# Reordering the first steps, the layer change and the end of a two-layer conditioned attention kernel

## The chip, the cores and the metric

The kernel runs on one core of a Trainium2 chip. The metric is the time of one execution in microseconds (us) on the device, the median of several runs. A profiled execution of the same program gives the trace from which all rows below are read.

## What is computed

`x` has shape (32, 128, 512): 32 sequences of 128 tokens with 512 features, in float32. Two layers follow each other, each with its own weights (16 heads of 32 in layer 0, 8 heads of 64 in layer 1). Of one layer:

```python
xn = layernorm(x) * norm_scale + norm_bias
q, k, v = xn @ Wq + bq, xn @ Wk + bk, xn @ Wv + bv
k, v = masked(k), masked(v)
q = softmax(q, within each head)          # over the head's features
k = softmax(k, over the 128 tokens)
attn = einsum('bhse,bhsd->bhed', k, v)
y = einsum('bhtd,bhed->bhte', q, attn)
scale, shift = split(silu(cond) @ film_W + film_b)     # cond: (32, 1024)
h = (layernorm(y) * film_norm_scale + film_norm_bias) * (1 + scale) + shift
x = x + silu(h) @ W_out + b_out
```

All large products run as three float32 products of high and low parts (`WH*XH`, `WL*XH`, `WH*XL`), so that each projection of one sequence is 12 matmuls of 128x512.

## The kernel before

One *step* is one sequence of one layer; there are 64 (0 to 31 in layer 0, 32 to 63 in layer 1). `x` stays in SBUF (`X`). Every engine has its own program, written out by hand as calls of small helpers (`keys(i)`, `values(i)`, `queries(i)`, `attention(j)`, `mix(j)`, `output(o)` on TensorE, and so on); semaphores tie them together. **The order of the calls on an engine is the order of the work**: an instruction that waits holds up everything behind it on its engine. Steps 5 to 30 and 34 to 61 run in loops of `even_step` and `odd_step`; steps 0 to 4, the change of layer (31 to 33) and the end (62, 63) are written out call by call.

What a step does, engine by engine: TensorE makes keys, values and queries; ScalarE keeps the keys in `SK` (`keep_keys`); VectorE takes the maxima over tokens of the keys of two steps (`key_maxima`, and `row_maxima`, which writes `NM`). SyncE sends `NM` to memory (`write_max`, `k_maxima<-NM`) and reads it back on all 128 partitions (`spread_max`, `MX<-k_maxima`, 512 KB); GpSimd subtracts it (`shift_keys`), ScalarE takes the exponential (`exp_k`), and TensorE can do `attention`. VectorE scales its result (`scale_heads`, `HT`), GpSimd puts it on a block diagonal (`heads`, `ATT`), and TensorE multiplies the queries with it (`mix`). The result is normalised (`mixed`, `root_y`, `norm_y`), turned by a DMA to memory and back (VectorE `turn_y`, SyncE `write_qy`/`read_qy`, `qy_turned`, `QT`; the queries travel in the same buffers), passed through `film` on ScalarE and `h_mul` on VectorE, split in two parts (`h_high` on ScalarE, `h_low` on GpSimd) and multiplied with the output weights (`output`). `add_bo` on GpSimd adds the output bias to `X`. The inputs of a pair of steps are normalised on ScalarE (`norm_x`, which needs `stat_x` on VectorE and `root_x` on GpSimd), turned by a DMA (`write_x`, `read_x`, `x_turned`, `XT`), and split (`x_turned` on ScalarE, `x_low` on GpSimd). The tiles `XS` and `QS` are what VectorE turned; they are free again when their DMA to memory has landed.

Weights are split in two parts by `split_high(w, chunks)` on ScalarE and `split_low` on VectorE or GpSimd; `w` is 0 to 3 for keys, values, queries and output of layer 0, 4 to 7 for layer 1. The weights of layer 1 come through one buffer, `STAGE`, chunk by chunk: a chunk is loaded (`load_second`) once the chunk before it has been split (`low_w`). `load_w(3)` brings the output weights of layer 0 (`in_wo`, 1 MB) and `load_film(0)` and `load_film(1)` the two halves of its conditioning weights (`in_film`, 2 MB each). They stand on SyncE's queue with the small transfers of each step. The product with the condition is `conditioning(n)`, `conditioning_sums(n)` and `conditioning_fold(n)`; `conditioning_fold` multiplies by `FOLD`, which `start()` on VectorE makes, with the head masks `DG`.

## Time and profile before

| | us |
|---|---|
| median of 3 runs | 910.99 (910.52 to 911.63) |
| the profiled execution | 909.31 |
| its span in the trace | 907.5 |
| TensorE busy | 847.9 |
| VectorE busy | 679.1 |
| GpSimd busy | 615.1 |
| ScalarE busy | 553.3 |

The profiled execution's time is 1.8 us above its span, and the median of the runs 1.7 us above that time. A timeline row gives the start and the duration of an instruction, and in brackets how long its engine had been idle before it and what ended that. "issue" there means that the trace names no other engine for the end of the wait. Where durations of matmuls are given, they overlap a little: twelve matmuls of 128x512 take 2.7 to 2.9 us when the granted clock is 1.00 (2.4 GHz) and some 5 us when it is 0.50 (1.2 GHz).

### The profile page before, as it was taken

The page shows a single profiled execution, that of the slowest core. Times are in us where ns is not written, and L with a number is a line of the kernel's source. Part 1 is how long each engine was busy: PE and PEld are TensorE (multiplying, and loading weights), DVE is VectorE, ACT ScalarE, POOL GpSimd, SP SyncE. Part 2 cuts the span into 40 slices and gives each one's busy share as a digit, 9 for nine tenths or more (in the row PEclk, how much of TensorE's full clock was granted, in tenths as well). Part 3 has the DMA queues.
Part 4 walks back from the last instruction along what each step waited for, and adds up shares of the span by engine and source line. Part 5 has one row for each costly group of instructions (what it writes and reads, how often), then busy time and mean ns, then how long its engine had stood idle before and what let it go on. Part 6 is the DMA issues. An engine that isn't in the chain of part 4 may idle for free.

```text
span 907.5 us, 18202 instructions
## 1 busy us (share of the span) xinstructions
PE 847.9 (93%) x5923; PEld 690.2 (76%) x5923; DVE 679.1 (75%) x1367; ACT 553.3 (61%) x994; POOL 615.1 (68%) x833
## 2 busy tenths in 40 slices
PE   8967799999999999999966989999999999999997
PEld 7645578787878877888745878888878787887876
DVE  6945568878878797888675678778877777877765
ACT  6245456666666666666663666666676666666653
POOL 2356457777767777777645787778776777777661
PEclk9988889999999999999989999999999999999999
DMA  9725246554555655444374345445454555445331
GB/s 349 239 90 164 93 135 207 191 182 164 183 191 163 209 186 178 149 153 149 119 222 135 96 141 187 159 168 174 159 170 139 174 172 178 157 170 186 117 106 59
DMA packets 94307, 148.85 MB, mean 164 GB/s; under 512 B 10990, under 2 KB 63590, under 8 KB 94214
## 3 DMA queue, kind: packets, MB, share of 16 engines
q1 hardware_dynamic: 93584, 146.97, 49.2%
q8 instruction: 48, 0.79, 0.4%
q10 hardware_dynamic: 630, 0.73, 0.2%
q14 instruction: 45, 0.37, 0.1%
HBM read 91.43 MB, written 56.23 MB: 163 GB/s over the span
## 4 chain that ended last, share of the span: by engine, by line
PE 59%; POOL 10%; DMA 9%; issue 8%; DVE 7%; ACT 5%; SPq 2%; POOLq 0%; ACTq 0%; DVEq 0%
PE PS L1126 51%; PE PS L1221 4%; DMA qy_turned<-QS 3%; DMA QT<-qy_turned 2%; PE PS L1196 2%; POOL SK L651 2%; ACT Z L854 2%; DMA X<-in_wq 1%; POOL XL L644 1%; POOL X L628 1%; SPq L448 1%; POOL SQ L635 1%; DMA MX<-k_maxima 1%; POOL RSY L593 1%; DMA k_maxima<-NM 1%
## 5 line engine op out<-in xcount | busy, mean ns | idle before, releaser
L854 ACT ACTIVATE Z<-QT,FC,FA 128x128 f32<-128x128 f32 x240 | 99.0, 483 | 74.8 <-DMA QT<-qy_turned 74.8
L1126 PE MATMUL PS<-WH_o,HH 128*128 128x512 f32 x248 | 101.1, 408 | 18.2 <-issue 18.2
L673 POOL TENSOR_TENSOR HL<-H,HH 128x512 fp32r<-128x512 f32 x60 | 77.9, 1298 | 57.1 <-ACT HH L896 55.6
L665 POOL TENSOR_TENSOR ATT<-HT,DG 128x256 f32<-128x256 f32 x124 | 76.8, 640 | 57.8 <-DVE HT L1596 30.0
L1126 PE MATMUL PS<-WH_v,XH 128*128 128x512 f32 x256 | 104.8, 409 | 9.9 <-DVE VV L1626 8.9
L1126 PE MATMUL PS<-WH_k,XH 128*128 128x512 f32 x256 | 107.0, 418 | 4.7 <-POOL XL L644 2.9
L1126 PE MATMUL PS<-WH_q,XH 128*128 128x512 f32 x256 | 101.1, 395 | 2.4 <-DVE SQ L1610 2.4
L1126 PE MATMUL PS<-WL_v,XH 128*128 128x512 f32 x256 | 101.8, 398 | 0.0
L1126 PE MATMUL PS<-WH_v,XL 128*128 128x512 f32 x256 | 101.6, 397 | 0.0
L1126 PE MATMUL PS<-WL_k,XH 128*128 128x512 f32 x256 | 101.2, 395 | 0.0
L1126 PE MATMUL PS<-WH_k,XL 128*128 128x512 f32 x256 | 100.8, 394 | 0.0
L1126 PE MATMUL PS<-WL_q,XH 128*128 128x512 f32 x256 | 99.9, 390 | 0.0
L1126 PE MATMUL PS<-WH_q,XL 128*128 128x512 f32 x256 | 99.7, 389 | 0.0
L1126 PE MATMUL PS<-WH_o,HL 128*128 128x512 f32 x248 | 98.8, 398 | 0.0
L1126 PE MATMUL PS<-WL_o,HH 128*128 128x512 f32 x248 | 98.7, 398 | 0.0
L644 POOL TENSOR_TENSOR XL<-XF,XH 128x512 fp32r<-128x512 f32 x60 | 77.6, 1294 | 30.7 <-ACT XH L922 29.1
L651 POOL TENSOR_TENSOR SK<-SK,MX 128x512 f32<-128x512 f32 x64 | 81.5, 1295 | 16.1 <-DMA MX<-k_maxima 16.0
L818 ACT ACTIVATE SK<-SK 128x512 f32<-128x512 f32 x64 | 40.3, 632 | 79.7 <-POOL SK L651 79.5
L635 POOL TENSOR_TENSOR SQ<-SQ,QM 128x512 f32<-128x512 f32 x64 | 67.9, 1061 | 29.5 <-DVE QM L1614 28.1
L823 ACT ACTIVATE YN<-YN,NBY,RSY 128x512 f32<-128x512 f32 x61 | 49.8, 816 | 61.0 <-POOL NBY L616 61.0
L628 POOL TENSOR_TENSOR X<-X,BB 128x512 f32<-128x512 f32 x64 | 82.6, 1292 | 2.3
L1221 PE MATMUL PS<-ATT,EQ 128*128 128x132 f32 x512 | 70.5, 282 | 13.1 <-issue 9.5
(174 smaller groups left out, 2060.2 us busy)
## 6 DMA issues: line engine op xcount, KB each, us to landing
qy_turned<-QS SPq DMA_DIRECT2D x60, 512.0 KB, 3.1
QT<-qy_turned SPq DMA_DIRECT2D x240, 128.0 KB, 2.9
MX<-k_maxima SPq DMA_DIRECT2D x32, 512.0 KB, 3.6
x_turned<-XS SPq DMA_DIRECT2D x30, 512.0 KB, 2.7
XT<-x_turned SPq DMA_DIRECT2D x120, 128.0 KB, 2.9
out_x<-X SPq DMA_DIRECT2D x31, 256.0 KB, 2.9
X<-in_x SPq DMA_DIRECT2D x11, 512.0 KB, 4.3
X<-in_film SPq DMA_DIRECT2D x2, 2048.0 KB, 13.0
```

The lines of the kernel that those rows point to most:

```text
L628: eng.tensor_tensor(X[:, b, :], X[:, b, :], BB[:, 2, :], ALU.add).then_inc(pool_bo, 1)
L635: eng.tensor_tensor(sq, sq, QM[:, 0:D // w].unsqueeze(2).to_broadcast([P, D // w, w]), ALU.subtract)\
L644: eng.tensor_tensor(XL[g % 2][:, dst, :], XF0[:, :, :], XH[g % 2][:, dst, :].bitcast(F32), ALU.subtract).then_inc(pool_xl, 1)
L651: eng.tensor_tensor(sk, sk, MX[:, i % 2, :], ALU.subtract).then_inc(pool_kn, 1)
L665: last = eng.tensor_tensor(dst, src.to_broadcast([P, 2, P // w, w]), here.to_broadcast([P, 2, P // w, w]), ALU.mult)
L673: eng.tensor_tensor(hl_of(o), h_of(o), hh_of(o).bitcast(F32), ALU.subtract).then_inc(pool_hl, 1)
L818: eng.activation(sk, sk, ACT.Exp).then_inc(act_ek, 1)
L823: eng.activation(y, y, ACT.Identity, bias=NBY[:, :], scale=RSY[:, :]).then_inc(act_yn, 1)
L854: z = eng.activation(z_of(o)[:, c * P:c * P + P].rearrange("p (q n) -> p q n", q=Q), src, ACT.Identity, bias=FC[l][:, c, b:b + 1], scale=F ...
L1126: mm = eng.matmul(dst, left[a](c), right[b](c), start=(c == 0 and a + b == 0), stop=(c == C - 1 and a == 1))
L1196: mm = eng.matmul(out_[f:f + 32, c, :], ks, v[:, (c * P + f) // w, :], start=True, stop=True, tile_position=(0, f))
L1221: mm = eng.matmul(bank(B_Y + c // 2, (c % 2) * W, W), EQ[:, c * P:c * P + P], ATT[:, c // 2, (c % 2) * W:(c % 2 + 1) * W], start=True, sto ...
```

## The change

Only the order of calls changes, in four places, and one wait is new. In the steady loops two things change, and both only in the last even step of layer 0 (`s == B - 2`, step 30): the splitting of the key weights of layer 1 is called there, not behind it.

* **First steps.** On SyncE `load_film(1)` and `load_w(3)` move behind `write_max(0)`, `write_x(2)` and `spread_max(0)`; `write_max(1)` moves ahead of `read_qy(3)`. On VectorE `queries(0)` moves ahead of the key maxima, `start_cond()` ahead of the statistics, and `start()` far back. `FOLD` is therefore made before `DG`, and `conditioning_fold(0)` waits for it. On ScalarE `exp_q(0)`, `x_turned(4)`, `values(3)` and `keep_keys(4)` move forward. On GpSimd the `add_bo` calls move back.
* **Layer change.** ScalarE, GpSimd, VectorE and SyncE get new orders for steps 31 to 33. TensorE keeps its order.
* **End.** TensorE does `output(59)` ahead of `mix(62)` and `output(60)` ahead of `mix(63)`; VectorE parts `h` of step 60 and scales the heads of step 63 ahead of `mixed(62)`.

```diff
@@ SyncE, first steps
             write_qy(1)
-            load_film(1)
             read_qy(1)
+            write_max(0)
+            write_x(2)
+            spread_max(0)
+            load_film(eng, 1)
             wait_split(0)
-            load_w(3)
-            write_max(0)
-            spread_max(0)
-            write_x(2)
+            load_w(eng, 3)
+            read_x(2)
             write_qy(2)
-            read_x(2)
             read_qy(2)
             write_qy(3)
             write_x(3)
+            write_max(1)
             read_qy(3)
-            write_max(1)
+            spread_max(1)
             read_x(3)
-            spread_max(1)
@@ VectorE, first steps
+            queries(0)
             key_maxima(0)
             key_maxima(1)
-            queries(0)
+            values(0)
+            start_cond()
+            turn_queries(0)
             stat_x(4)
-            values(0)
-            turn_queries(0)
             stat_x(5)
             stat_x(6)
-            start()
-            start_cond()
...
             stat_x(8)
+            queries(2)
             stat_x(9)
-            queries(2)
+            start()
@@ TensorE, conditioning_fold(n)
                 if n > 0:
                     eng.wait_ge(dve_film, n)
+                else:
+                    eng.wait_ge(dve_diag, 2)
@@ GpSimd, first steps
-            add_bo(2)
             h_low(0)
-            add_bo(3)
-            add_bo(4)
             x_low(6)
             queries(4)
+            add_bo(1)
+            add_bo(2)
+            add_bo(3)
             heads(2)
+            add_bo(4)
@@ ScalarE, layer change (in step 30, and behind it)
+                if s == B - 2:
+                    for c in range(C):
+                        split_high(4, [c])
                 x_turned(s + 2)
...
             exp_q(29)
-            keep_keys(32)
             norm_x(35)
             split_high(5, [0])
+            norm_y(28)
             split_high(5, [1])
+            keep_keys(32)
+            split_high(5, [2])
+            split_high(5, [3])
+            values(31)
             exp_k(30)
             exp_k(31)
-            split_high(5, [2])
-            split_high(5, [3])
             keep_keys(33)
+            film(28)
             norm_y(29)
-            film(28)
             h_high(28)
@@ VectorE, layer change
+            for c in range(C):
+                split_low(eng, 5, [c])
             add_x(27)
-            split_low(eng, 5, [0])
             mixed(29)
-            split_low(eng, 5, [1])
-            split_low(eng, 5, [2])
-            split_low(eng, 5, [3])
             turn_queries(31)
             scale_heads(30)
-            key_maxima(33)
             turn_y(29)
             h_mul(28)
+            key_maxima(33)
             values(32)
             split_low(eng, 6, [0])
             split_low(eng, 6, [2])
+            values(33)
             stat_x(37)
             stat_x(38)
-            values(33)
             add_x(28)
@@ TensorE, end
             turn_y(t9)
+            output(LAST_Y - 1)
             mix(t1)
+            attention(t2)
+            turn_queries(t2)
             turn_y(t0)
-            output(LAST_Y - 1)
-            turn_queries(t2)
-            attention(t2)
+            output(t9)
             mix(t2)
             turn_y(t1)
-            output(t9)
```

How the orders stand, at three places. SyncE's queue in the first steps, from the first turned queries on (`MX<-k_maxima` is `spread_max`), before:

```order
L433 DMA qy_turned<-QS 512x1x128
L399 DMA X<-in_film0 128x8x512
L448 DMA QT<-qy_turned 32x4x128 x4
L391 DMA STAGE<-in_wo0 128x4x512
L454 DMA k_maxima<-NM 32x32
L461 DMA MX<-k_maxima 128x1024
L415 DMA x_turned<-XS 128x1024
L433 DMA qy_turned<-QS 512x1x128
L423 DMA XT<-x_turned 32x4x256 x4
```

and now:

```order
L435 DMA qy_turned<-QS 512x1x128
L450 DMA QT<-qy_turned 32x4x128 x4
L456 DMA k_maxima<-NM 32x32
L417 DMA x_turned<-XS 128x1024
L463 DMA MX<-k_maxima 128x1024
L374 DMA X<-in_film0 128x8x512
L379 DMA STAGE<-in_wo0 128x4x512
L425 DMA XT<-x_turned 32x4x256 x4
L435 DMA qy_turned<-QS 512x1x128
```

The two weight loads (3 MB) stood ahead of both transfers of the maxima; now they stand behind them and ahead of the reading of the turned inputs.

GpSimd at the layer change, from `heads(30)` to `x_low(35)` (`XL<-XF,XH` is `x_low`, `HL<-H,HH` is `h_low`, `VEX`/`RSX`/`NBX` are `root_x`, `SQ<-SQ,QM` is `queries`), before:

```order
L665 TENSOR_TENSOR ATT<-HT,DG 128x256 x2
L590 TENSOR_SCALAR VEX<-MVX 128x1
L593 TENSOR_TENSOR RSX<-VEX,half 128x1
L606 TENSOR_SCALAR NBX<-MVX,RSX 128x1
L673 TENSOR_TENSOR HL<-H,HH 128x512
L356 TENSOR_TENSOR WL_q<-STAGE,WH_q 128x512
...
L673 TENSOR_TENSOR HL<-H,HH 128x512
L644 TENSOR_TENSOR XL<-XF,XH 128x512
L635 TENSOR_TENSOR SQ<-SQ,QM 128x512
L644 TENSOR_TENSOR XL<-XF,XH 128x512
```

and now:

```order
L667 TENSOR_TENSOR ATT<-HT,DG 128x256 x2
L675 TENSOR_TENSOR HL<-H,HH 128x512
L356 TENSOR_TENSOR WL_q<-STAGE,WH_q 128x512 x2
L646 TENSOR_TENSOR XL<-XF,XH 128x512
L592 TENSOR_SCALAR VEX<-MVX 128x1
L595 TENSOR_TENSOR RSX<-VEX,half 128x1
L608 TENSOR_SCALAR NBX<-MVX,RSX 128x1
L646 TENSOR_TENSOR XL<-XF,XH 128x512
```

`h_low(28)` no longer stands behind `root_x(37)`, and both `x_low(34)` and `x_low(35)` stand ahead of `h_low(29)` and of the queries of steps 32 and 33.

VectorE at the end, from the heads of step 62 on, before:

```order
L1584 TENSOR_TENSOR ATT<-PS,RE 64x2x2x64 x2
L1644 RECIPROCAL RQ<-PS 128x16
L1651 TENSOR_TENSOR XT<-PS,RQ 128x512
L1656 BN_STATS BNY<-XT 128x6
L1658 BN_AGGR MVY<-BNY 128x2
L1664 SCALAR_TENSOR_TENSOR H<-H,Z 128x512
L1671 CAST HH<-H 128x512
L1672 TENSOR_TENSOR HL<-H,HH 128x512
```

and now:

```order
L1588 TENSOR_TENSOR ATT<-PS,RE 64x2x2x64 x2
L1668 SCALAR_TENSOR_TENSOR H<-H,Z 128x512
L1675 CAST HH<-H 128x512
L1676 TENSOR_TENSOR HL<-H,HH 128x512
L1704 TENSOR_TENSOR X<-PS,X 128x512
L1583 RECIPROCAL RE<-PS 128x4
L1588 TENSOR_TENSOR ATT<-PS,RE 64x2x2x64 x2
L1648 RECIPROCAL RQ<-PS 128x16
```

`mixed(62)` (`RQ`, `XT`, `BNY`, `MVY`) moved behind the parts of `h` of step 60 (`HH`, `HL`) and the heads of step 63.

## Rows read from the trace of the kernel before

**Rows 1.** Busy time by stretch: start:end, length, busy us (instructions), clock, DMA
```profile
0.00:115.00 115.00, 87.47 (x539) 68.54 (x540) 71.48 (x156) 51.72 (x89) 55.34 (x83) 0.91 0.56 188
165.00:440.00 275.00, 270.94 (x1972) 220.79 (x1972) 222.14 (x447) 178.19 (x320) 203.71 (x273) 1.00 0.54 175
440.00:540.00 100.00, 81.25 (x527) 63.64 (x527) 69.33 (x138) 58.33 (x106) 66.06 (x84) 0.94 0.47 150
```

**Rows 2.** TensorE, first steps: start, duration, instruction, [idle before <- releaser]
```profile
55.70 0.79 PE L1126 MATMUL PS<-WH_v,XH 128*128 128x512 f32 x1 [5.35 <-DVE VV L1626]
...
68.93 1.17 PE L1221 MATMUL PS<-ATT,EQ 128*128 128x132 f32 x8 [1.68 <-ACT EQ L834]
...
86.72 0.77 PE L1126 MATMUL PS<-WH_o,HH 128*128 128x512 f32 x1 [5.55 <-issue]
...
114.78 2.10 PE L1221 MATMUL PS<-ATT,EQ 128*128 128x132 f32 x8 [5.62 <-issue]
```

**Rows 3.** SyncE's issues in the first steps, same columns
```profile
30.14 0.62 SPq L399 DMA_DIRECT2D X<-in_film  x1
34.92 1.76 SPq L448 DMA_DIRECT2D QT<-qy_turned  x4
...
43.63 0.34 SPq L461 DMA_DIRECT2D MX<-k_maxima  x1
...
76.04 0.34 SPq L461 DMA_DIRECT2D MX<-k_maxima  x1
```

**Rows 4.** Chain of waits: start, duration, what
```profile
37.28 6.33 DMA k_maxima<-NM
43.63 4.22 DMA MX<-k_maxima
...
86.72 5.11 PE PS L1126 x12
...
123.91 8.37 PE PS L1126 x36
```

**Rows 5.** DMA issues by line: count, KB each, median us to landing
```profile
X<-in_film SPq DMA_DIRECT2D x1, 2048.0 KB, 16.0
...
X<-in_film SPq DMA_DIRECT2D x1, 2048.0 KB, 9.9
...
k_maxima<-NM SPq DMA_DIRECT2D x3, 4.0 KB, 2.9
```

**Rows 6.** GpSimd before output(0), columns as in group 2
```profile
81.61 2.48 POOL L651 TENSOR_TENSOR SK<-SK,MX 128x512 f32<-128x512 f32 x2 [5.78 <-DMA MX<-k_maxima]
84.05 1.27 POOL L628 TENSOR_TENSOR X<-X,BB 128x512 f32<-128x512 f32 x1
85.35 1.27 POOL L673 TENSOR_TENSOR HL<-H,HH 128x512 fp32r<-128x512 f32 x1
```

**Rows 7.** TensorE at the layer change
```profile
467.62 0.79 PE L1126 MATMUL PS<-WH_v,XH 128*128 128x512 f32 x1 [3.60 <-DVE VV L1626]
...
475.32 0.47 PE L1126 MATMUL PS<-WH_o,HH 128*128 128x512 f32 x1 [2.22 <-issue]
...
483.46 0.50 PE L1126 MATMUL PS<-WH_q,XH 128*128 128x512 f32 x1 [1.39 <-DVE SQ L1610]
...
488.39 0.47 PE L1126 MATMUL PS<-WH_o,HH 128*128 128x512 f32 x1 [1.92 <-issue]
...
496.73 0.47 PE L1126 MATMUL PS<-WH_k,XH 128*128 128x512 f32 x1 [2.90 <-POOL XL L644]
```

**Rows 8.** GpSimd at the layer change
```profile
472.63 0.22 POOL L590 TENSOR_SCALAR VEX<-MVX 128x1 f32<-128x1 f32 x1 [7.12 <-DVE MVX L1496]
...
473.95 1.27 POOL L673 TENSOR_TENSOR HL<-H,HH 128x512 fp32r<-128x512 f32 x1
...
495.21 1.26 POOL L644 TENSOR_TENSOR XL<-XF,XH 128x512 fp32r<-128x512 f32 x1
```

**Rows 9.** TensorE at the end
```profile
890.37 2.10 PE L1221 MATMUL PS<-ATT,EQ 128*128 128x132 f32 x8 [2.52 <-issue]
```

More of the change, by code:

```diff
@@ L1937, in _ @@
             mixed(30)
+            h_mul(29)
             scale_heads(31)
+            queries(32)
+            turn_y(30)
             turn_x(36)
-            queries(32)
-            h_mul(29)
             turn_queries(32)
-            turn_y(30)
             queries(33)
```

130 lines of the change are left out of this document (62 added, 68 removed).

## The prediction

> **What bounds the kernel now.** I read the busy times by stretch first, and look for idle time of the busiest engine. TensorE works 270.94 of 275 us in the steady steps of layer 0, at full clock [rows 1]. Nothing in the loops can be won by an order. But in the first 115 us it is idle for 115 - 87.47 = 27.5 us, and from 440 to 540 us for 18.8 us, and in both stretches the granted clock is below 1.00 as well [rows 1]. So the kernel is bound by TensorE, and what can be won lies where TensorE waits: at the start, at the layer change and a little at the end. Since TensorE is full in between, I take it that a microsecond won at the start reaches the end whole. The second view is TensorE's timeline with the idle time in brackets, the third the chain of waits, which says what ended each wait.
>
> **First steps: the first maxima.** Before `values(3)` TensorE stands idle for 5.35 us [rows 2]. It waits for VectorE, which waits for ScalarE, which waits for the first shifted keys, which wait for `MX<-k_maxima`. That transfer is issued at 43.63, because the 4 KB of `k_maxima<-NM` before it took 6.33 us to land [rows 4]; the median of the first three such transfers is 2.9 us [rows 5]. In front of it on the queue were 2 MB of film weights, issued at 30.14 [rows 3] and landed 9.9 us later [rows 5], and 1 MB of output weights behind them. The change takes both away from there. The new issue time: SyncE's four reads of the turned queries start at 34.92 because they wait for VectorE's `x_low(3)` [rows 3]. With `start()` gone from ahead of it and `queries(0)` earlier I get `x_low(3)` done 1.1 us earlier (an estimate from the length of those calls). So the reads go out from 33.8 to 35.6, the 4 KB at 35.9, they land within 2.9 us, at 38.8 at the latest, and `MX` is issued at about 38.4, which is 5.2 us earlier. Its landing took 4.22 us [rows 4]. Now 512 KB of `x_turned` go out just ahead of it; the second one, also behind other transfers, was issued at 76.04 and landed at 81.6, 5.5 us later [rows 3, 6]. I take 4.8 us, the middle. **Term 1: -5.2 + 0.6 = -4.6 us at `values(3)`.** The bounds are -4.0 and -5.5. What is late next is nothing: the statistics, `keep_keys(3)` and `key_maxima(3)` follow the same exponential as before.
>
> **What the 3 MB now hold up.** They are issued at 38.7 and stand ahead of `read_x(2)`, `write_qy(2)` and `read_qy(2)`. Between them 3.25 MB took from 30.14 to 43.4 before, some 13 us, so with 4.75 MB now queued from 37.5 on I have all landed by 52 to 55. ScalarE needs the output weights at `split_high(3)` and the turned inputs at `x_turned(4)`. VectorE needs `write_qy(2)` landed for `turn_queries(2)`, and `conditioning(0)` and `values(3)` stand behind that. In my replay these are due at 51 (ScalarE), 52 (VectorE), and the first thing that TensorE wants of them, `mix(1)`, at about 62.8. So the cost is nothing as long as they land by 57. If the film weights take the 16.0 us that the first half took [rows 5], they land at 54.7, the output weights 3.4 us later, and `write_qy(2)` at 58.5. Then `mixed(0)` is 2 to 3 us late and so is everything behind it. A row shows that the 4 KB, issued last, landed no earlier than the 3 MB ahead of them [rows 4]. The Trainium skill ("DMA: Bandwidth & Descriptors", section "Queues, rings and completion order") gives the reason: the semaphore increment of a transfer lands on each DMA engine only after every earlier write of that engine. By that rule `write_qy(2)` inherits the delay that the maxima lose, and the trace agrees.
>
> **First steps: the second maxima.** `output(0)` waits 5.55 us [rows 2], for `h_low(0)` on GpSimd, which runs from 85.35 to 86.6, behind two `shift_keys` that wait for the second `MX` until 81.6, and behind one `add_bo` of 1.27 us [rows 6]. Four things change. All of it starts 4.6 us earlier (term 1). `write_max(1)` goes out ahead of the four reads of `read_qy(3)`, which take 1.76 us to issue [rows 3], and does not land behind them, which I put at 1.0 us. The `add_bo` between is gone, 1.3 us. The landing of `MX` is perhaps 0.5 us shorter. **Term 2: -1.8 - 1.0 - 1.3 - 0.5 = -4.6 us, so `output(0)` starts at 86.7 - 9.2 = 77.5.** TensorE gets there at about 75, so a wait of 2 to 3 us is left. The `add_bo` calls moved behind `queries(4)` now stand ahead of `heads(2)`, 3.8 us for three; `mix(2)` comes some 9 us after the start of `output(0)`, and that just covers them. The wait of 5.62 us before `mix(3)` [rows 2] follows from the third maxima, whose order is the old one; it stays.
>
> **The clock.** After each wait of more than 5 us twelve matmuls take 5.11 us, where they take 8.37 / 3 = 2.79 us in the steady steps [rows 4]. The wait of 1.68 us [rows 2] is not followed by such a loss. Both waits that I shorten end at 2 to 3 us, between these two. The loss goes with neither or with both: 0 to -4.6 us. I take 0 and keep -4.6 for the range.
>
> **Layer change.** `values(33)` starts at 467.62 after 3.60 us of idle time, for VectorE's `values(32)` [rows 7]. In the new order that instruction stands behind `turn_y(29)`, `h_mul(28)` and `key_maxima(33)`, and ScalarE does `film(28)` ahead of `norm_y(29)`, which waits for `read_qy(31)`. My replay has it only 0.8 us earlier, so this wait gets no better. What is won comes after. `h_low(28)` at 473.95 stood behind `root_x(37)`, for which GpSimd idled 7.12 us until VectorE's statistics at 472.63 [rows 8]; now it is done before `values(33)` ends, and the 2.22 us before `output(28)` go [rows 7]. `x_low(35)` at 495.21 held `keys(34)` back by 2.90 us [rows 7, 8]; it stood behind the queries of step 33. It moves ahead of them by far, and the 2.90 go. The 1.92 us before `output(29)` [rows 7] fall as well, and so does a smaller wait between it and `keys(34)`, before `mix(31)`: from 488.39 to 496.73 are 8.3 us [rows 7], of which `output(29)` and `mix(31)` work some 4.2 and `keys(34)` waits 2.90, which leaves 1.3. They fall, since `h_low(29)` no longer waits behind the queries of step 32 and ScalarE no longer stands between. The 1.39 us before `queries(33)` [rows 7] stay: `queries(32)` on VectorE still stands behind `mixed(30)`, `h_mul(29)` and `scale_heads(31)`. **Term 3: -0.8 - 2.2 - 1.9 - 1.3 - 2.9 = -9.1 us.** `keys(34)` ran behind its wait at the low clock. By [rows 4] twelve such matmuls lose up to 5.11 - 2.79 = 2.3 us; the first of this group still takes 0.47 us and not 0.79 [rows 7], so I take 1.6 of it, which goes when no wait stands before it. The key weights of layer 1 split in step 30 put 2.2 us of ScalarE ahead of `x_turned(32)`, and 1.3 of GpSimd ahead of `x_low(33)`; `film(27)` waits longer for its data than that, so ScalarE's part is covered, and GpSimd's makes `keys(32)` some 0.5 us later, which is already in the -0.8. **Term 4: -1.6. Together -10.7,** bounds -4 and -13.
>
> **End.** TensorE idles 2.52 us before `mix(63)` [rows 9], and in two shorter gaps ahead of it. `output(59)` and `output(60)` move into these gaps, 2.8 us each. But `mixed(62)` on VectorE moves behind the parts of `h`, so that `norm_y(62)` and `turn_y(62)` come about 0.4 us later, and the last two outputs are bound by ScalarE's `film` behind that. **Term 5: -1.0 us,** bounds -2.5 and +1.5.
>
> **Sum.** -4.6 - 4.6 - 10.7 - 1.0 = -20.9 us: a span of 886.6 for 907.5, and 910.99 - 20.9 = **890 us** for the median, which lies 3.5 us above the span before and should after.
>
> **Rivals.** (a) *The layer change gives little.* `values(33)` could come later than I have it: the reads of `read_qy(31)` now stand on SyncE behind `load_second(6, [0])`, which waits for `split_low(5, [0])` on VectorE, which waits for `turn_y(28)`. Each microsecond there is one at `values(33)`. If terms 3 and 4 halve or vanish, the time is 895 to 901. (b) *The clock comes back in full* and the maxima land at their shortest: 880 to 885. For it: after 1.68 us of waiting the clock held. Against it: TensorE's waits in the first steps come one upon the other. (c) *The weights are late*, the 16.0 us case above: 2 to 4 us lost of terms 1 and 2, 893; it does not turn the sign. (d) *The steady steps fall into another rhythm*, slower than before. With the chain shifted against the film loads and `load_x` on SyncE, one wait per pair of steps could come later. There are some 26 pairs; from 20.9 / 26 = 0.8 us per pair on the change is a loss, and with 1.0 us the time is 916. For it: 4.1 us of idle time in 275 show that the loops have waits already [rows 1]. Against it: the loops are unchanged and each pair hands the next the same distances. (e) *Nothing moves* since TensorE's idle time only shifts from one wait to the next (`mix(3)` takes up what `output(0)` gives): 909 to 913.
>
> **Chances.** Forecast (885 to 895) 0.55, (a) 0.20, (b) 0.10, (c) within the forecast, (d) 0.07, (e) 0.03, and 0.05 for a gain of 2 to 9 us left over by several small losses. The range of 8 in 10 takes the forecast, most of (a) and half of (b): 882 to 902. A measurement of this kernel can tell about 0.2% (1.8 us) from no change: faster by more than that 0.90, same 0.03, slower 0.07.
>
> **What would show it.** In the trace after: the first `k_maxima<-NM` lands within 3 us and `MX` before 44; `values(3)` starts near 51 and `output(0)` near 77.5; the two film and output loads land by 55; `values(33)` starts as long before its old place as the start has won, plus 0.8 us; no wait before `output(28)` and `keys(34)`; the clock of `keys(34)` is 1.00. The forecast is wrong if `mix(3)` is less than 7 us earlier, if `keys(34)` is less than 14 us earlier, or if the two stretches of steady steps are longer than before.

## The result and the profile after

| | before | after |
|---|---|---|
| median | 911.31 (910.52 to 912.34, 4 runs) | 896.11 (895.47 to 900.09, 4 runs) |
| the profiled execution | 909.31 | 895.47 |
| its span | 907.5 | 893.7 |

The change makes the kernel 1.6% faster: the ratio is 0.984, 95% interval 0.981 to 0.987. Measured a second time beside the kernel before, it came out at 0.987 (0.982 to 0.993; fifth run below). The forecast was 890.0 us in a range of 882 to 902. So sign and range held, but the gain is some 15 us and not 21. Span against span it is 13.8 us where the sum had 20.9.

Busy time by stretch, as [rows 1]: start:end, length, then busy us and instructions of TensorE, its weight loads, VectorE, ScalarE, GpSimd, and the granted clock, the share and the rate of the DMAs.

```profile
0.00:115.00 115.00, 92.38 (x561) 73.70 (x562) 74.80 (x162) 52.42 (x90) 57.59 (x87) 0.91 0.58 192
165.00:440.00 275.00, 272.40 (x1979) 221.84 (x1978) 224.76 (x452) 183.46 (x331) 203.08 (x273) 1.00 0.52 170
440.00:540.00 100.00, 86.72 (x568) 70.10 (x567) 74.58 (x151) 60.63 (x109) 75.10 (x97) 0.95 0.51 169
```

TensorE gained 4.9 us of work in the first 115 us and 5.5 us in the stretch of the layer change, and the steady steps are as full as before. Where it waits is seen in its timeline. First the same four places as [rows 2], then the layer change, as [rows 7], with `keys(32)` ahead:

```profile
53.31 0.50 PE L1128 MATMUL PS<-WH_v,XH 128*128 128x512 f32 x1 [2.98 <-DVE VV L1630]
...
62.84 1.14 PE L1223 MATMUL PS<-ATT,EQ 128*128 128x132 f32 x8 [0.23 <-issue]
...
80.58 0.76 PE L1128 MATMUL PS<-WH_o,HH 128*128 128x512 f32 x1 [5.95 <-issue]
...
443.11 0.47 PE L1128 MATMUL PS<-WH_k,XH 128*128 128x512 f32 x1 [2.66 <-issue]
...
463.66 0.80 PE L1128 MATMUL PS<-WH_v,XH 128*128 128x512 f32 x1 [5.95 <-DVE VV L1630]
...
476.81 0.50 PE L1128 MATMUL PS<-WH_q,XH 128*128 128x512 f32 x1 [1.67 <-DVE SQ L1614]
```

`values(3)` waits 2.98 us for 5.35, and `mix(1)` next to nothing. But `output(0)` waits as long as before, `keys(32)` has a new wait, and `values(33)` waits longer than before, 5.95 for 3.60. `output(28)`, `output(29)` and `keys(34)` wait no more.

**One landmark table for all traces.** Here is the start of `keys(i)` on TensorE (the 12i-th matmul with key weights), in us, as distances, since the first of them starts anywhere from 13.1 to 16.4:

| | keys(0) starts | 0 to 6 | 6 to 30 | 30 to 34 | 34 to 62 | 62 to the end | keys(0) to the end |
|---|---|---|---|---|---|---|---|
| before | 13.1 | 103.4 | 309.3 | 70.9 | 359.6 | 51.2 | 894.4 |
| after | 15.3 | 95.3 | 308.4 | 64.3 | 358.5 | 52.0 | 878.4 |
| e1 first steps undone | 13.8 | 104.0 | 308.1 | 64.4 | 358.2 | 52.0 | 886.7 |
| e2 layer change undone | 13.7 | 95.7 | 307.7 | 72.6 | 357.1 | 51.1 | 884.2 |
| e3 end undone | 16.1 | 96.1 | 307.2 | 67.4 | 355.2 | 50.2 | 876.1 |
| e4 weights early | 13.5 | 102.3 | 309.8 | 68.0 | 356.3 | 51.8 | 888.2 |
| e5 after, again | 13.5 | 95.6 | 307.9 | 64.5 | 358.1 | 51.8 | 877.9 |
| e6 40 fillers twice | 13.4 | 97.8 | 313.8 | 64.8 | 359.1 | 52.2 | 887.7 |
| e7 values(32) early | 13.4 | 95.7 | 307.7 | 64.4 | 357.4 | 51.6 | 876.8 |
| e8 both orders | 15.1 | 96.3 | 308.0 | 63.0 | 357.2 | 52.1 | 876.6 |
| e9 20 fillers twice | 16.4 | 94.0 | 307.7 | 68.6 | 354.9 | 51.3 | 876.5 |
| e10 half the end | 13.4 | 96.9 | 305.1 | 66.6 | 358.9 | 53.1 | 880.7 |
| e11 read first | 14.7 | 96.4 | 307.8 | 63.1 | 361.2 | 51.8 | 880.3 |
| e12 combined | 15.1 | 94.3 | 308.3 | 60.3 | 357.2 | 51.4 | 871.4 |

From `keys(0)` on the change is worth 894.4 - 878.4 = 16.0 us: 8.1 in the first steps, 0.9 in the steady steps of layer 0, 6.6 at the layer change, 1.1 behind it, and -0.8 at the end. The span shows 2.2 us less, as `keys(0)` itself was late in that execution.

The table also shows how far a section moves when nothing in it has changed. With the new first steps 0 to 6 takes 95.3 to 96.9 us (after, e2, e3, e5, e7, e8, e10, e11), so they are worth 6.5 to 8.1 us. With the new layer change 30 to 34 takes 64.3 to 64.5 us in three traces (after, e1, e5) and 66.6 to 68.0 in three others (e3, e4, e10), so it is worth 2.9 to 6.6 us against the 70.9 of the kernel before. A difference of 1 us between two traces proves little; what parts the two groups of the layer change is shown at the ninth run below.

### The profile page after: what moved, and what is told of

The parts are those of the page before. It is cut to its first block, busy times and chain, and to the rows that moved or that the text cites. A ratio compares the mean times of both kernels' runs of the same rounds, so it can differ in the third digit from the quotient of the medians.

```text
span 893.7 us, 18205 instructions
## 1 busy us (share of the span) xinstructions
PE 844.3 (94%) x5923; PEld 688.0 (77%) x5923; DVE 679.9 (76%) x1367; ACT 553.8 (62%) x994; POOL 615.6 (69%) x833
## 4 chain that ended last, share of the span: by engine, by line
PE 63%; DMA 9%; issue 7%; DVE 6%; POOL 6%; ACT 5%; SPq 3%; POOLq 0%; ACTq 0%; DVEq 0%
PE PS L1128 54%; PE PS L1223 4%; DMA QT<-qy_turned 3%; DMA qy_turned<-QS 3%; PE PS L1198 2%; ACT Z L857 2%; SPq L450 1%; DMA x_turned<-XS 1%; SPq L425 1%; DMA MX<-k_maxima 1%; POOL SK L653 1%; POOL SQ L637 1%; POOL HL L675 1%; DMA STAGE<-in_wk 1%; POOL RSY L595 1%
## 5 line engine op out<-in xcount | busy, mean ns | idle before, releaser
L857 ACT ACTIVATE Z<-QT,FC,FA 128x128 f32<-128x128 f32 x240 | 98.9, 483 | 72.6 <-DMA QT<-qy_turned 72.6
L1668 DVE SCALAR_TENSOR_TENSOR H<-H,Z 128x512 f32<-128x512 f32 x62 | 45.3, 731 | 54.4 <-ACT H L862 53.6
## 6 DMA issues: line engine op xcount, KB each, us to landing
X<-in_film SPq DMA_DIRECT2D x2, 2048.0 KB, 13.1
```

What stands on the lines that cost most here:

```text
L857: z = eng.activation(z_of(o)[:, c * P:c * P + P].rearrange("p (q n) -> p q n", q=Q), src, ACT.Identity, bias=FC[l][:, c, b:b + 1], scale=F ...
L1668: eng.scalar_tensor_tensor(out=h, in0=h, scalar=1.0, in1=z_of(o), op0=ALU.add, op1=ALU.mult).then_inc(dve_h, 1)
```

## The experiments

The ratio is to the kernel before, measured beside it, with its 95% interval. Single executions of any of these kernels differ by some 1%, so small effects are read from the traces.

### The four parts, one at a time

`e1_first_undone`, `e2_layer_undone` and `e3_end_undone` are the changed kernel with the order of before in one of the three places, on all engines. `e4_weights_early` undoes only this:

```diff
@@ SyncE, against the changed kernel
             write_qy(1)
+            load_film(eng, 1)
             read_qy(1)
+            wait_split(0)
+            load_w(eng, 3)
             write_max(0)
             write_x(2)
             spread_max(0)
-            load_film(eng, 1)
-            wait_split(0)
-            load_w(eng, 3)
             read_x(2)
```

> The changed kernel with its first steps in the order of before on all engines; the layer change and the end stay changed. My theory, from the trace of the changed kernel: the new first steps bring 6 to 7 us, since values(3) moved from 55.7 to 53.3 us and mix(3) from 114.8 to 108.8 us, and the steady steps carry that on unchanged; so 896.1 + 6.4 = 902.5 us, 901 to 904. The forecast on record said 9.2 us for this part (905.3 us). Rival, the steady steps absorb what the start gains, so that the layer change alone made the result: 896 to 898 us.

> The changed kernel with its layer change in the order of before; first steps and end stay changed. My theory, from the trace: mix(28) is 6.9 us earlier and keys(34) 15.1 us, so the part is worth 7.5 to 8 us: 904 us, 902.5 to 905. The forecast on record said 10.7 us (906.8 us). Rival, the two parts share their gain, since GpSimd's split of the second key weights, 2.45 us here, belongs to the early arrival and not to the order: then the part is worth up to the whole 10.7 us or over (907 us and above) or, the other way, under 5 us (below 901 us).

> The changed kernel with its last steps on TensorE and VectorE in the order of before. My theory, from the trace: mix(61) is 14.6 us earlier and the last instruction 13.9, so the new end costs 0.7 us here, and with the old one the time is 895.4 us (894 to 896.5). The forecast on record said that it brings 1.0 us: 897.1 us. Rival, the 0.7 us is not of the order but of the GpSimd instructions there, which took longer in that execution: then the time is 897 us.

> The changed kernel with one thing put back: SyncE issues the second film weights and the output weights (3 MB together) ahead of the first maxima's write again. My theory: the spread of the first maxima then waits for the 3 MB in the queue as in the kernel before, values(3) starts 4 to 5 us later (57.8 us for 53.3), TensorE's clock is half there again, and the time is 896.1 + 3 to 5 = 900 us (898.5 to 902). Rival, transfers collide instead: in the changed kernel the third write of queries takes 9.8 us to land behind the 3 MB, where it took 6.9 us before, so the gain at values(3) is given back at the exponentials of the queries and the two orders are within 1.5 us of each other (895 to 897.5).

Measured: e1 902.7 us, 0.993 (0.990 to 0.996); e2 905.1 us, 0.995 (0.992 to 0.998); e3 894.9 us, 0.985 (0.979 to 0.991); e4 900.6 us, 0.990 (0.984 to 0.995). Before took 908.7 us there.

**The parts add.** In the table e1 loses just the 8 us of the first steps and keeps the 64.4 us of the layer change, and e2 does the reverse. The rival that the steady steps absorb the start is out: 6 to 30 takes 307 to 310 us in twelve of the fourteen traces. Against the changed kernel's 0.984, e1's ratio puts the first steps at 0.9% (8 us) and e2's the layer change at 1.1% (9.6 us); against its second measurement, 0.987, it is 0.6% and 0.7% (5 and 7 us). The times thus agree with the table, but they are no finer than it.

**The weights are most of the first part.** e4's SyncE timeline shows what they do to the spread of the first maxima:

```profile
36.62 0.50 SPq L456 DMA_DIRECT2D k_maxima<-NM  x1
37.51 0.34 SPq L417 DMA_DIRECT2D x_turned<-XS  x1
45.14 0.34 SPq L463 DMA_DIRECT2D MX<-k_maxima  x1
```

With 3 MB ahead of it the read back of the maxima is issued 8.5 us after the write of 4 KB. In the changed kernel it is 2.1 us:

```profile
37.68 0.43 SPq L456 DMA_DIRECT2D k_maxima<-NM  x1
39.29 0.34 SPq L417 DMA_DIRECT2D x_turned<-XS  x1
39.74 0.37 SPq L463 DMA_DIRECT2D MX<-k_maxima  x1
40.15 0.73 SPq L374 DMA_DIRECT2D X<-in_film  x1
41.04 0.81 SPq L379 DMA_DIRECT2D STAGE<-in_wo  x1
42.36 3.84 SPq L425 DMA_DIRECT2D XT<-x_turned  x4
46.24 0.61 SPq L435 DMA_DIRECT2D qy_turned<-QS  x1
56.06 1.74 SPq L450 DMA_DIRECT2D QT<-qy_turned  x4
```

`keys(6)` comes 6.7 to 7.0 us later behind `keys(0)` in e4 than in e5 and after, where the whole part brings 7.8 to 8.1. By the times it is less clear: 0.990 for 0.984 and 0.987, with intervals that meet. The collision that the rival named is there (the last two lines: the third write of the queries, issued at 46.24, is landed at 56.06 only, and VectorE idles 2.12 us for it), but it costs little, as `mix(1)` hardly waits. In the kernel before this write landed 5.1 us after its issue; the 6.9 us of the expectation run to the issue of the read behind it.

**The end did not decide.** The order of before took 50.2 us from `keys(62)` to the end in e3, 51.2 in the kernel before, and 51.4 and 51.8 in two kernels below. The new one took 51.1 to 52.2 (nine traces). That is 0.5 us in favour of the old order by the middle values, with ranges that overlap. The ratio of e3 is that of the changed kernel.

### The changed kernel again, and fillers

`e5_after_again` is the changed kernel. `e6_fillers` adds matmuls that nobody reads, to keep TensorE's clock up; nothing is left out:

```diff
@@ TensorE
             values(4)
+            keep_busy(B_O, 40)
             output(0)
...
             values(32)
+            eng.wait_ge(dve_x, 28)
+            keep_busy(B_O, 40)
             values(33)
```

> The changed kernel itself, once more, beside the kernel before. Its first execution had TensorE's first key product 2.1 us later than before's (15.3 for 13.1 us), because a first weight chunk and ScalarE's split of it were late. My theory: that is a difference of launches, since the six traces so far put it anywhere from 13.1 to 16.1 us, whatever the order; so values(3) starts 38 us behind keys(0) again, mix(3) 93.5 to 94.5 us behind it (before: 101.7), and the ratio to the kernel before is 0.984 (894.3 us where before takes 908.7). Rival, the new order delays the first steps itself: keys(0) again over 1.5 us later than in the other kernels.

> The changed kernel with 40 matmuls of the identity, 128 columns each, added on TensorE ahead of output(0)'s wait (5.9 us idle, output(0) then at half clock: 5.3 us for 12 matmuls, 2.9 at full clock) and ahead of values(33)'s (5.9 us idle, 5.0 us for 12). They take some 0.11 us each, 4.5 us, inside the wait, and write a bank that is free. My theory: the waits end when they did, the clock stays at its upper level, output(0) and values(33) each take 2 to 2.4 us less and the kernel is 3 to 4.5 us faster than the changed one. Rival, the 3 us are absorbed, because the instructions behind wait for VectorE and ScalarE anyway (behind output(0) attention(2), keys(5); behind values(33) output(28)): under 1.5 us. Other rival: the fillers delay the instruction that they stand before, and the kernel is slower.

e5: 897.6 us for 909.1, 0.987 (0.982 to 0.993), and its profiled execution, with a span of 891.4, was the shortest of its four. `keys(0)` started at 13.5 us, as early as before. **So the late start was the launch.** In the first profile of after the chain of waits begins with the second transfer of key weights, landed at 7.56 (5.94 in e5, 5.56 in the kernel before):

```profile
1.63 5.93 DMA STAGE<-in_wk
```

e6: 906.2 us, 0.997 (0.994 to 1.000), 8.6 us slower than e5. My price for a filler was wrong, since each of these f32 matmuls is two records: 80 of them took 9.1 us and outlasted the wait. It says something all the same: `output(0)` was 3.8 us later than in e5 and ran at full clock (2.98 us for 4.6), `mix(3)` only 2.1 us later, and then 6 us went in the steady steps 6 to 30 (313.8 us). This is the only run in which these steps ran slower, rival (d) of the prediction; in e10 they ran 3 us faster (305.1). What held them I didn't find. `e9_fillers_short` has 20 instead of 40:

> The fillers again, 20 instead of 40 at either place: the run with 40 showed that each takes 0.22 us (80 records, 9.1 us), not 0.11, so that they outlasted both waits by over 3 us. 20 take 4.5 us and fit into the 5.8 to 7 us waits. My theory now: output(0) and values(33) run at full clock (3.0 us each for 5.3 and 5.0), keys(6) comes up to 2.3 us earlier behind keys(0) than the changed kernel's 95.3 to 95.6 us, and keys(34) another 1 to 2, so the time is 2 to 4 us below the changed kernel's. Rival, from the run with 40: full clock at output(0) only lengthens the next waits (mix(3) waited 7.0 us for 5.6), keys(6) is within 0.7 us of 95.5, and the steady steps between keys(6) and keys(30), 308 us in seven kernels, took 313.8 with the fillers; so the same time or more.

e9: 893.8 us for 908.5, 0.983 (0.976 to 0.990). Ahead of `output(0)` the fillers work: `output(0)` takes 3.0 us, and `keys(6)` comes after 94.0 us, for 95.3 to 96.9 without them (94.3 in e12, which has them too). At the layer change they don't:

```profile
443.94 0.47 PE L1128 MATMUL PS<-WH_k,XH 128*128 128x512 f32 x1 [2.76 <-issue]
...
456.76 4.62 PE L1325 MATMUL PS<-ident 128*128 128x128 f32 x40
...
465.12 0.50 PE L1128 MATMUL PS<-WH_v,XH 128*128 128x512 f32 x1 [3.73 <-DVE VV L1633]
```

TensorE is idle 3.73 us behind them all the same, and the twelve matmuls of `values(33)` took 4.4 us. From 30 to 34 it is 68.6 us, 4 longer, and from 34 to 62 it is 3 shorter. So it was in e3 and e4 too (67.4 and 68.0, then 355.2 and 356.3): some 2 to 3 us lost at the layer change came back behind it, in three traces, but not in e10 (66.6, then 358.9).

What is lost can be read. In these four traces (e3, e4, e9, e10) `queries(33)` waits 2.45 to 2.60 us, where it waits 1.67 in after, e1 and e5, and its twelve matmuls then take 4.4 to 4.6 us for 3.0. It waits for VectorE, and there one addition of 32x32 elements (`NM<-NM`, of `row_maxima(16)`) took 1.17 to 1.32 us for 0.18. e3, TensorE, VectorE and GpSimd:

```profile
478.75 0.50 PE L1128 MATMUL PS<-WH_q,XH 128*128 128x512 f32 x1 [2.60 <-DVE SQ L1614]
...
473.63 1.32 DVE L1574 TENSOR_TENSOR NM<-NM,BKT 32x32 f32<-32x32 f32 x1
...
473.62 1.28 POOL L646 TENSOR_TENSOR XL<-XF,XH 128x512 fp32r<-128x512 f32 x1 [1.10 <-issue]
```

and after, VectorE and GpSimd:

```profile
472.61 0.18 DVE L1574 TENSOR_TENSOR NM<-NM,BKT 32x32 f32<-32x32 f32 x1
...
472.62 1.34 POOL L646 TENSOR_TENSOR XL<-XF,XH 128x512 fp32r<-128x512 f32 x1 [1.09 <-issue]
```

In e3, e4, e9 and e10 GpSimd's `x_low(35)` had started 0.01 to 0.17 us before the addition, and the addition ended with it. In after, e1, e5 and e6 it started 0.01 to 0.03 us behind the addition, which took 0.18 us. So some 2.5 us at the layer change hang on which of two engines comes first by a hundredth of a microsecond, whatever the order under test. What comes back behind it is TensorE's idle time between `keys(34)` and `keys(62)`: 2.9, 3.6 and 3.3 us in e3, e4 and e9, and 6.6 and 5.2 in after and e5 (5.8 in e10). Why it does so in three traces and not in the fourth stays open.

### What holds the layer change

`e7_values32_early` moves one call on VectorE, and `e8_both_orders` has this and GpSimd's too:

```diff
@@ VectorE (e7, e8)
             scale_heads(30)
+            values(32)
             turn_y(29)
             h_mul(28)
             key_maxima(33)
-            values(32)
@@ GpSimd, even_step(30) and behind it (e8)
                     split_low(eng, 4, [1])
+                    x_low(33)
                 for n in stats_at(s):
                     root_x(n)
...
             even_step(30)
-            x_low(33)
-            h_low(27)
             root_y(28)
+            h_low(27)
             heads(29)
```

> The changed kernel with VectorE's values(32), the addition that empties the bank that TensorE's values(33) wants, ahead of turn_y(29), h_mul(28) and key_maxima(33) instead of behind them. My theory, from the changed kernel's trace: its input is ready at 457.7 us, but it starts at 462.9 because VectorE idles 3.96 us at turn_y(29), whose norm_y(29) stands behind film(28) on ScalarE. With it ahead, TensorE's values(33) starts at 458.5 to 459 instead of 463.7 and at full clock (3 for 5 us); output(28) then waits for GpSimd's h_low(28) till about 463.5 instead of starting at 468.5; keys(34) comes 3 to 5 us earlier (479 for 483.2) and the time is 3 to 5 us lower. Rival, the layer change hangs on film(28) and its transfer (landed at 457.3) and not on values(33): output(28), queries(33) and keys(34) keep their times within 1 us.

> e7 with GpSimd's order changed too: x_low(33) right behind the second key weights' split instead of behind root_x(35) and root_x(36), and root_y(28) ahead of h_low(27). My theory: x_low(33) starts at 438.9 instead of 441.6, keys(32) 2.4 us earlier (440.7 for 443.1) and at a higher clock, norm_y(28) and with it the write and the read of the queries and film(28) 1 to 1.3 us earlier; so another 1 to 2.5 us below e7. Rival, keys(32) only starts earlier to wait later: same as e7 within 0.7 us.

In the trace of after the wait of `values(33)` reads as follows, first ScalarE, then VectorE:

```profile
457.32 1.65 ACT L857 ACTIVATE Z<-QT,FC,FA 128x128 f32<-128x128 f32 x4 [2.03 <-DMA QT<-qy_turned]
459.00 0.63 ACT L862 ACTIVATE H<-Z 128x512 f32<-128x512 f32 x1
459.53 0.80 ACT L826 ACTIVATE YN<-YN,NBY,RSY 128x512 f32<-128x512 f32 x1
```

```profile
460.36 0.71 DVE L1535 STREAM_TRANSPOSE QS<-YN 128x512 f32<-128x512 f32 x1 [3.96 <-ACT YN L826]
461.00 0.65 DVE L1668 SCALAR_TENSOR_TENSOR H<-H,Z 128x512 f32<-128x512 f32 x1
461.57 0.70 DVE L1559 STREAM_TRANSPOSE KT<-SK 128x512 f32<-128x512 f32 x1
462.30 0.69 DVE L1562 TENSOR_REDUCE PM<-KT 128x16 f32<-128x512 f32 x1
462.92 0.68 DVE L1630 TENSOR_TENSOR VV<-PS,BB 128x512 f32<-128x512 f32 x1
```

`film(28)` waits for its transfer until 457.32, `norm_y(29)` stands behind it, VectorE's `turn_y(29)` behind that, and three calls later comes `values(32)`, whose input was there at 457.7.

e7: 892.7 us for 909.1, 0.982 (0.977 to 0.988). e8: 892.2 us, 0.981 (0.976 to 0.986). `values(33)` starts at 456.6 in e7 for 462.6 in e5. But `output(28)` is 4.3 us earlier, `queries(33)` 1.7, and `keys(34)` 0.4. **So my theory was wrong, and the rival right at `keys(34)`** (for `output(28)` and `queries(33)` it had said within 1 us): the wait at `values(33)` was only where TensorE showed it. What takes its place is TensorE's `queries(33)`, which waits 2.6 us for VectorE's `queries(32)`, behind `h_mul(29)`, behind ScalarE's `film(29)`, and then runs at a granted clock of 0.66 (4.4 us for 3.0).

e8's GpSimd shows the second point, the wait of `keys(32)`. The changed kernel first:

```profile
436.44 2.45 POOL L356 TENSOR_TENSOR WL_k<-STAGE,WH_k 128x512 fp32r<-128x512 f32 x1
438.97 0.22 POOL L592 TENSOR_SCALAR VEX<-MVX 128x1 f32<-128x1 f32 x1
...
441.63 1.27 POOL L646 TENSOR_TENSOR XL<-XF,XH 128x512 fp32r<-128x512 f32 x1
```

The split of the key weights that the change put into step 30 takes 2.45 us, and the two `root_x` behind it 2.6 us more, before `x_low(33)`. With `x_low(33)` ahead of them:

```profile
436.83 2.47 POOL L356 TENSOR_TENSOR WL_k<-STAGE,WH_k 128x512 fp32r<-128x512 f32 x1
439.25 1.30 POOL L646 TENSOR_TENSOR XL<-XF,XH 128x512 fp32r<-128x512 f32 x1
440.63 0.22 POOL L592 TENSOR_SCALAR VEX<-MVX 128x1 f32<-128x1 f32 x1
```

`keys(32)` then waits no more and comes 21.3 us behind `keys(30)` for 24.4 in e7; of this 1.4 us is left at `keys(34)` (63.0 for 64.4), and the times of e7 and e8 are the same within their spread.

### Half of the end, and the read first

`e10_end_half` is the changed kernel with the old order of the last steps on VectorE alone. `e11_read_first` is e8 with the old end on both engines and this:

```diff
@@ SyncE, layer change
             write_x(17)
-            load_second_bias(1, dve_q)
+            read_qy(31)
             load_second_bias(0, dve_v)
             load_second(eng, 6, [0])
-            read_qy(31)
+            load_second_bias(1, dve_q)
             load_second(eng, 6, [1])
```

> The changed kernel with VectorE's last steps in the order of before, TensorE's in the new one. From keys(62)'s start to the end of the span the new order took 51.6 to 52.2 us in six kernels (51.1 in another), the order of before 51.2 and 50.2. My theory: the loss is VectorE's mixed(62), which stands behind h_mul(60) in the new order: mix(62) on TensorE ends at 869.5 us, mixed(62) starts at 874.5, and turn_y(62) waits for it until 879.0. With VectorE's old order turn_y(62) no longer waits, and keys(62) to the end takes 49.5 to 50.5 us: 1.5 to 2 us under the changed kernel. Rival, TensorE's order costs it, because mix(63) stands behind output(60), which waits for ScalarE's film(60): then it takes 51.5 to 52 us as before.

> The two orders of the eighth run (VectorE's values(32) early, GpSimd's x_low(33) and root_y(28) early) and the old end, and one thing more: SyncE issues the read of the turned queries (28 to 31) ahead of the second biases and the first chunk of the second query weights instead of behind them. The seventh and eighth run showed that an earlier values(33), 6 us, and an earlier keys(32) leave keys(34) where it was: ScalarE starts film(28) when that read has landed (456.1 to 457.0 us, 6.7 us from its issue) and is then busy without a gap for 15 us, and queries(33) waits for VectorE behind film(29). My theory: the read then lands 3 to 4 us after its issue, film(28) starts 2 to 3 us earlier, keys(30) to keys(34) takes 60 to 61 us for 63.0, and with the old end (1 to 2 us) the time is 0.975 of the kernel before or a little less (885 to 888 us where before takes 909). Rival, VectorE's values(32) now waits for its bias instead, or film(28) for VectorE's part: 63 us as in the eighth run, and a ratio of 0.979.

e10: 894.4 us for 908.5, 0.984 (0.979 to 0.990). The end took 53.1 us, the longest of all. My theory of VectorE's `mixed(62)` falls:

```profile
868.85 0.26 DVE L1648 RECIPROCAL RQ<-PS 128x16 f32<-128x16 f32 x1 [2.44 <-PE PS L1223]
...
878.14 0.26 DVE L1648 RECIPROCAL RQ<-PS 128x16 f32<-128x16 f32 x1 [3.42 <-PE PS L1223]
```

`mixed(62)` does start at 868.9 (874.5 in the changed kernel), but VectorE then waits 3.42 us for TensorE's `mix(63)`, which stands behind `output(60)`. The two orders belong together. As I read it, the new order fills gaps ahead of `mix(63)` and takes away the work that stood behind it, when the last chain through VectorE and ScalarE runs; no run tried that apart.

e11: 890.3 us for 908.5, 0.980 (0.974 to 0.987). `film(28)` starts 1.7 us earlier behind `keys(32)` than in e8, not 2 to 3, as ScalarE's `keep_keys(33)` ahead of it now waits for TensorE; and 30 to 34 stays 63.1. `queries(33)` waits 4.7 us instead, since VectorE's `queries(32)` stands behind `h_mul(29)`, which waits for `film(29)`. The rival's numbers hold nearly, 63 us and a ratio of 0.979, but for another reason than the two that it gave.

### All of it, and the next link

`e12_combined` is e11 with 20 fillers ahead of `output(0)` and

```diff
@@ VectorE
             mixed(30)
+            queries(32)
             h_mul(29)
             scale_heads(31)
-            queries(32)
             turn_y(30)
```

> The eleventh run's kernel (values(32) early on VectorE; x_low(33) and root_y(28) early on GpSimd; the old end; the read of the turned queries ahead of the second biases) with two things more: VectorE's queries(32) ahead of h_mul(29) and scale_heads(31), and 20 matmuls of the identity ahead of output(0). My theory: in the eleventh run queries(33) on TensorE waited 4.7 us for queries(32) on VectorE, which waited for h_mul(29), this for ScalarE's film(29) and this for its transfer; with queries(32) ahead, queries(33) starts 2 to 3 us earlier behind keys(32), and keys(30) to keys(34) takes 60 to 61.5 us for 63.1. The fillers bring keys(6) 94 to 94.5 us behind keys(0) for 95.4. Together the kernel is 4 to 6 us below the changed one: a ratio to the kernel before of 0.976 to 0.980. Rival, the next wait takes over again (output(29) for h_low(29)), or the steady steps behind take back what the layer change gains, as in the runs of the old end and of the short fillers, where a layer change longer by 3 to 4 us was followed by steady steps shorter by as much: then 0.980 to 0.984, as the changed kernel.

e12: 892.1 us for 909.6, 0.981 (0.978 to 0.983). The ratio misses the expected 0.976 to 0.980 and lies in the range of the rival, 0.980 to 0.984. The trace of its fastest but one execution does what was expected of it:

```profile
458.41 0.50 PE L1128 MATMUL PS<-WH_v,XH 128*128 128x512 f32 x1 [0.79 <-DVE VV L1631]
...
461.68 0.47 PE L1128 MATMUL PS<-WH_o,HH 128*128 128x512 f32 x1 [0.26 <-issue]
...
470.07 0.50 PE L1128 MATMUL PS<-WH_q,XH 128*128 128x512 f32 x1 [1.67 <-DVE SQ L1615]
```

60.3 us from `keys(30)` to `keys(34)` and 94.3 to `keys(6)`, and 871.4 us from `keys(0)` to the end, 6.5 to 7 less than the changed kernel. **The 2.8 us below e11 from 30 to 34 (60.3 for 63.1) come from the new place of `queries(32)`,** as the fillers stand 350 us earlier: behind `keys(32)`, `film(28)` and `film(29)` start just as in e11 (14.6 and 28.2 us), and `queries(33)` waits 1.67 us for 4.73. The kernel's ratio is below those of the changed kernel, 0.984 and 0.987, and no better than e8's 0.981 and e11's 0.980. The intervals meet (0.983 is the upper end of one, 0.981 and 0.982 the lower ends of the others), and the two kernels were never measured side by side. That it beats the changed kernel is likely, by 3 to 6 us, and not proved. Which of its six parts count in the time was not tried apart.

## Why the prediction was right in sign and too large in size

**Term 1, the first maxima (-4.6 us): right in size, in part by luck.** `values(3)` comes 38.1 us behind `keys(0)` (53.31 - 15.26), and 42.6 before. That is -4.5. The 4 KB landed within 2.1 us, `MX` 4.8 us after its issue, both as put. The film and output weights landed by 54.1 (52.0 with the late launch, 2.1 us, taken off), within the 52 to 55. e4 shows that the weights are most of the cause. But less the launch `MX` was issued 6.0 us earlier, not 5.2, and landed 5.5 us earlier (5.2 in e5). Of that 0.7 to 0.9 us was lost behind it, where I had said that nothing is late next: ScalarE's `keep_keys(3)` now waits for TensorE.

```profile
50.49 0.69 ACT L815 ACTIVATE SK<-PS,MK 128x512 f32<-128x512 f32 x1 [1.18 <-PE PS L1198]
```

**The clock (0 us, range to -4.6): it varies from one execution to the next.** After the same 2.98 us of waiting the twelve matmuls of `values(3)` took 3.0 to 3.1 us in three traces (after, e2, e7) and 4.2 to 5.5 in eight; before it was some 5.2. In the profiled execution of after the granted clock was 1.00 there, in e5 it fell while they ran. So 0 to -2.2 us: a value of 0 was not wrong for most executions, and the median holds both kinds. Before `output(0)` the wait stayed and the clock with it at its lower level. The stretches in the trace of after, `values(3)`, `output(0)` and `keys(32)`; the clock is the third number from the end:

```profile
53.00:57.00 4.00, 3.69 (x20) 3.19 (x20) 1.82 (x6) 2.88 (x6) 2.43 (x3) 1.00 0.51 121
...
81.00:86.00 5.00, 5.00 (x31) 3.51 (x34) 0.00 (x0) 1.10 (x2) 4.43 (x4) 0.54 0.65 175
...
443.00:448.00 5.00, 4.89 (x15) 3.88 (x16) 1.65 (x4) 1.61 (x3) 4.65 (x8) 0.66 0.21 82
```

**Term 2, the second maxima (-4.6 us more, -9.2 in all): mis-sized.** `output(0)` came 7.3 to 8.3 us earlier behind `keys(0)` (e5 and after; 6.7 to 7.8 in the other traces with these first steps and no fillers), and the expected wait of 2 to 3 us was 5.8 to 6.0. The issue of the second `MX` moved by -7.4 in e5, which is the forecast's -4.6 - 1.8 - 1.0, and the `add_bo` is gone. What failed is its landing: I took 0.5 us off, but it rose from 5.5 to 6.5 us in e5 and 6.9 in after (69.76 to 76.6):

```profile
67.05 0.43 SPq L456 DMA_DIRECT2D k_maxima<-NM  x1
69.76 0.38 SPq L463 DMA_DIRECT2D MX<-k_maxima  x1
```

```profile
76.68 2.50 POOL L653 TENSOR_TENSOR SK<-SK,MX 128x512 f32<-128x512 f32 x2 [3.91 <-DMA MX<-k_maxima]
79.21 1.27 POOL L675 TENSOR_TENSOR HL<-H,HH 128x512 fp32r<-128x512 f32 x1
```

The wait did not shrink for a second reason: TensorE was at `output(0)` at 74.6 us in after and 74.1 in e5, which is 72.5 and 73.7 on the scale of the forecast (less the late launch), not 75. `mix(1)` had hardly waited. So `mix(3)` is 7.8 to 8.1 us earlier behind `keys(0)`, and not 9.2. The prediction called itself wrong under 7 us here and under 14 us at `keys(34)`. On the axis of the profiled execution of after both signs came: 6.0 us (114.78 and 108.82) and 13.5 (496.73 and 483.19). Behind `keys(0)`, without the late launch, they did not: 8.1 and 15.7 us, and 7.8 and 15.6 in e5.

**Terms 3 and 4, the layer change (-10.7 us): the large miss.** `keys(30)` to `keys(34)` shows -6.6 and -6.4, and with the next two steps, where the clock comes in, -7.2 and -7.0. All the waits that were to go went, and `keys(34)` ran at full clock, 2.98 us for 4.58 (term 4 right). The step that failed is the -0.8 at `values(33)`. Behind `keys(30)` it came 44.8 us (e5: 45.5) and 41.8 before, so it was +3.0 to +3.8 and not -0.8. Of this 2.5 to 2.9 us are there at `keys(32)` already, where I had put 0.5. Three prices failed. ScalarE's split of the key weights (2.2 us) I had called covered, since `film(27)` waits; but it stands ahead of `x_turned(32)`, and `film(27)` behind, so that `x_low(32)` comes 1.8 to 2.1 us later behind `keys(30)` (e5 and after). First the kernel before, then after:

```profile
438.76 1.29 POOL L644 TENSOR_TENSOR XL<-XF,XH 128x512 fp32r<-128x512 f32 x1 [0.93 <-ACT XH L922]
...
433.88 1.58 POOL L646 TENSOR_TENSOR XL<-XF,XH 128x512 fp32r<-128x512 f32 x1 [3.01 <-ACT XH L925]
```

GpSimd's split took 2.45 us and not 1.3 (1.74 in the kernel before). And `root_x(35)` and `root_x(36)` were forgotten ahead of `x_low(33)`; they stood there before too, but GpSimd then idled 1.55 us behind them. `keys(32)` then ran at half clock (4.6 us for 3.6). e8 confirms the last one at `keys(32)`, but only 1.4 us of it reaches `keys(34)`.

The rest of the wait at `values(33)` is argued, not shown: `norm_y(29)` stands behind `film(28)`, whose transfer had landed at 457.3, while its own input was there at 456.4. Rival (a) had this place, and as its cause SyncE's read behind `load_second(6, [0])`. In the profile of after that was not what held the read:

```profile
450.84 0.33 SPq L365 DMA_DIRECT2D STAGE<-in_wq  x1
451.69 1.76 SPq L450 DMA_DIRECT2D QT<-qy_turned  x4
```

The write of the turned queries, issued at 447.14, had landed at 451.68 only. In e5 and e8 it landed after 2.6 us, and there the read did stand 1.5 and 1.7 us longer, behind the weight chunk. The range of rival (a), 895 to 901, has the measured time in it. But it spoke of terms 3 and 4 halved or gone. In after and e5 6.4 to 6.6 of the 10.7 us came; in e3, e4 and e10, where the addition on VectorE was held up, 2.9 to 4.3. And e11 shows that an earlier read alone gives nothing, since `keys(34)` stayed; what held it there was VectorE's `queries(32)` (e12), a wait that the forecast had put at 1.39 us before and after.

**Term 5, the end (-1.0 us): wrong, and small.** The end is some 0.5 us longer, if anything. I had counted the gaps that `output(59)` and `output(60)` fill, not that they may have covered a later wait: `turn_y(63)` started 5.9 us behind `mix(63)` in e3 (876.13 and 881.98) and 6.9 in the changed kernel (875.80 and 882.66). In the kernel before, with the old order, it was 7.0 (890.37 and 897.39), so this is not shown.

**What was not in the sum.** Steady steps, 0.9 and 1.1 us to the good, and the launch, 2.1 us to the bad in the profiled execution. Behind `keys(0)`, 8.1 for 9.2, 6.6 for 10.7, -0.8 for +1.0, and +2.0 unforeseen, give some 16 for 20.9. Rivals (d) and (e) did not occur in the changed kernel; the gain at the start arrived whole. Only terms 1 and 4 came as put; terms 2, 3 and 5 all brought less, and 2.0 us that no term had made up for some of it.

## What to carry to other kernels

A small transfer on which an exponential hangs should stand ahead of the megabytes on its queue: this alone was worth most of the gain of the first steps here (5.4 to 7.0 of 6.5 to 8.1 us at the sixth step). A wait on the busiest engine is where a delay shows, not where it comes from: taking away 6 us of wait at `values(33)` gave 0.4 us at `keys(34)` (e7), an earlier `film(28)` gave nothing either (e11), and 2.8 us came when VectorE's `queries(32)` no longer stood behind `h_mul(29)` (e12). Where a call is moved ahead on a helper engine, count the calls that stay between it and the consumer, at the duration that they have beside a busy neighbour. And before an order is judged by two traces, look whether a long instruction of one of them is an accident of who came first.
